# A fused transformer kernel: prologue written out, V's first half read later in its quarter, the attended rows' read signalled in halves

## The reference

```python
x = x + 0.5 * ffn(layernorm(x))
x = x + attn(layernorm(x))      # two K and V sets, 16 heads of 8 channels, state = product of K^T V, linear in the sequence
x = x + 0.5 * ffn(layernorm(x))

def ffn(x):                     # 16 heads of 64, 8 experts, the best 2 chosen per row and head
    q, k = x @ Wq[h], x @ Wk[h]
    w, sel = top_k(x @ Ws[h], 2);  mix = one_hot(sel) * sigmoid(w)
    v = sum_e mix[h, e] * (x @ Wv[e])
    attended = softmax(q * scale @ k.T) @ v
    mask = one_hot(top_k(x @ Wd[h], 2))
    return sum_h sum_e mask[h, e] * (attended[h] @ Wo[e].T)
```

## Time and profile before

| | |
|---|---|
| median of 3 runs | 2392.2 us (2389.46 to 2398.71) |
| the profiled execution | 2388.17 us, span 2386.4 us |
| TensorE, matmuls | 2293.9 us busy (96%), 49920 |
| TensorE, weight loads | 2148.7 us (90%) |
| VectorE | 2060.7 us (86%) |
| ScalarE | 1950.4 us (82%) |
| GpSimd | 1161.0 us (49%) |
| DMA, mean | 163 GB/s |
| granted TensorE clock | 0.998 |

### The profile page before, as it was taken

The page is one execution under the profiler, slowest core; times in us unless marked ns, Lnnn a source line. Parts: engine busy times, 40 slices in busy tenths (PEclk is TensorE's granted clock), DMA queues, the critical chain, the costliest instruction groups (busy, mean ns, idle before and its releaser), DMA issues.

```text
span 2386.4 us, 120494 instructions
## 1 busy us (share of the span) xinstructions
PE 2293.9 (96%) x49920; PEld 2148.7 (90%) x49920; DVE 2060.7 (86%) x3755; ACT 1950.4 (82%) x6053; POOL 1161.0 (49%) x1190
## 2 busy tenths in 40 slices
PE   3999999999999999999999999999999999999997
PEld 3899898999999999999999999999999999999897
DVE  5888888989889898888989888888888888898884
ACT  2888787888888888888888888888888888888885
POOL 3445555455455454454454454454454454554431
PEclk9999999999999999999999999999999999999999
DMA  4555555655555555556556556556556555556553
GB/s 122 160 171 154 147 161 149 171 164 169 163 164 170 167 168 168 161 164 174 162 166 173 162 164 178 163 164 173 166 165 175 162 168 165 169 163 172 161 166 103
DMA packets 660701, 388.23 MB, mean 163 GB/s; under 512 B 232512, under 2 KB 585664, under 8 KB 660160
## 3 DMA queue, kind: packets, MB, share of 16 engines
q1 hardware_dynamic: 659728, 379.67, 55.0%
q10 hardware_dynamic: 432, 0.85, 0.1%
HBM read 191.64 MB, written 188.74 MB: 159 GB/s over the span
## 4 chain that ended last, share of the span: by engine, by line
PE 86%; ACT 6%; issue 4%; DVE 2%; POOL 1%; DMA 0%; SPq 0%; ACTq 0%; DVEq 0%; POOLq 0%
PE psT L477 19%; PE psS L432 15%; PE psT L494 8%; PE psT L496 6%; PE psT L495 6%; PE psS L524 6%; PE psT L524 6%; PE psT L445 6%; PE psT L489 5%; PE psT L459 5%; ACT PB L812 5%; ACT PJ L853 1%; DVE NMAX L693 1%; PE psT L603 1%; PE psT L530 1%
## 5 line engine op out<-in xcount | busy, mean ns | idle before, releaser
L812 ACT ACTIVATE PB<-psS,NMAX 128x256 f32<-128x256 f32 x2048 | 943.5, 488 | 101.4 <-DVE NMAX L693 101.4
L477 PE MATMUL psT<-V,PT 128*64 128x64 f32 x16384 | 544.3, 224 | 22.9 <-issue 22.2
L477 PEld LDWEIGHTS psT<-V,PT 128*64 128x64 f32 x16384 | 505.3, 138 | 51.7 <-issue 26.5
L812 ACT ACTIVATION_READ_ACCUMULATOR PB<-psS,NMAX 128x1 f32 x2048 | 452.8, 221 | 0.0
L761 DVE TENSOR_TENSOR QK<-psT,QK 128x512 fp32r<-128x512 f32 x512 | 349.0, 688 | 119.0 <-ACT QK L820 112.4
L432 PE MATMUL psS<-QK 64*128 64x256 f32 x6144 | 442.8, 288 | 3.1 <-DVE PT L765 2.6
L820 ACT ACTIVATE QK<-psT 128x512 fp32r<-128x512 f32 x512 | 307.3, 602 | 164.8 <-PE psT L496 141.0
L432 PEld LDWEIGHTS psS<-QK 64*128 64x128 f32 x6144 | 393.5, 187 | 8.3 <-issue 4.7
L693 DVE TENSOR_REDUCE NMAX<-psS 128x2 f32<-128x512 f32 x512 | 329.6, 685 | 51.5 <-PE psS L432 48.1
L927 POOL TENSOR_TENSOR BT<-MT,diagv 128x1024 f32<-128x1024 f32 x128 | 304.5, 2379 | 110.4 <-DMA MT<-MIXd 106.3
L933 POOL TENSOR_TENSOR MB<-MASKT,diago 128x1024 f32<-128x1024 f32 x128 | 250.2, 1956 | 144.3 <-DVE GM L770 116.4
(11 more groups left out here) (121 smaller groups left out, 4777.9 us busy)
## 6 DMA issues: line engine op xcount, KB each, us to landing
Vd<-VM SPq DMA_DIRECT2D x512, 128.0 KB, 2.3
V<-Vd SPq DMA_DIRECT2D x512, 128.0 KB, 3.1
AOd<-AO SPq DMA_DIRECT2D x256, 256.0 KB, 2.7
AR<-AOd SPq DMA_DIRECT2D x256, 256.0 KB, 4.1
PJd<-PJ SPq DMA_DIRECT2D x64, 512.0 KB, 2.8
PR<-PJd SPq DMA_DIRECT2D x256, 128.0 KB, 2.5
MIXd<-MIX SPq DMA_DIRECT2D x64, 128.0 KB, 2.3
MT<-MIXd SPq DMA_DIRECT2D x64, 128.0 KB, 3.3
```

The costliest lines, as they stand in the source:

```text
L477: last = eng.matmul(M[64 * u:64 * u + 64, (t * NT + it) * DH:(t * NT + it + 1) * DH], PT[:, t, jt, cols], V[:, pm % 2, 4 * r + t, jt, :], ...
L812: eng.activation(PB[:, ab, j, it, :], psS[:, ab, j, it, :], ACT.Exp, bias=NMAX[:, ab, j, it:it + 1], accum_out=SUM[:, p % 2, it, 4 * r + t ...
```

## The change

Three things. First, the loops start at quarter 0, and each engine has the prologue written out in an order of its own (`AHEAD` gives the banks; 16 items, as before). Each constant has its own semaphore, the first inputs and weights are read ahead of the others, the work of sequences 0 to 2 is interleaved with the rounding of weights, and the first projections stand ahead of the first values. In GpSimd's prologue the mask's step comes after the mix. Second, in the fourth quarter SyncE's queue stores V's second half first, then waits for the product that TensorE computes in this quarter, reads V's first half, stores AO and then reads PR. Third, `s_ar` becomes two semaphores, one for each half of AR's four reads, and each half of `expand` waits for its own. New functions (`gates`, `choose`, `choose_second`, `store_mix` and others) hold the code that stood in the loops.

```diff
-        QUARTERS = range(-12, total + 6)
+        QUARTERS = range(total + 6)
...
+        AHEAD = [("xturn", 0), ("gates", 0), ("expert", 0, 0), ("expert", 0, 1), ("xturn", 1), ("gates", 1), ("qk", 0), ("qk", 1), ("xturn", 2),
+                 ("values", 0, 0, 0), ("values", 0, 0, 1), ("expert", 1, 0), ("values", 0, 1, 0), ("values", 0, 1, 1), ("expert", 1, 1), ("gates", 2)]
+        place = {item: k for k, item in enumerate(AHEAD)}
...
-            eng.dma_start(raw_g, WgT).then_inc(s_const, 16)
-            eng.dma_start(raw_q, WqT).then_inc(s_const, 16)
-            for dst, src in ((diagv, diagv_d), (diago, diago_d), (ramp, ramp_d), (headmask, heads_d), (awq, aWq), (awkv, aWkv), (awo, aWo)):
+            eng.dma_start(raw_g, WgT).then_inc(s_gload, 16)
+            eng.dma_start(ramp[:], ramp_d).then_inc(s_gload, 16)
+            eng.dma_start(X[:, 1].rearrange("p n c -> p (n c)"), x_rows(x, 1)).then_inc(s_x[1], 16)
+            eng.dma_start(raw_q, WqT).then_inc(s_qload, 16)
+            eng.dma_start(X[:, 2].rearrange("p n c -> p (n c)"), x_rows(x, 2)).then_inc(s_x[2], 16)
+            for dst, src in ((diagv, diagv_d), (diago, diago_d), (headmask, heads_d), (awq, aWq), (awkv, aWkv), (awo, aWo)):
                 eng.dma_start(dst[:], src).then_inc(s_late, 16)
...
+            eng.dma_start(X[:, 3].rearrange("p n c -> p (n c)"), x_rows(x, 3)).then_inc(s_x[3], 16)
...
+            store_experts(0)
+            load_experts(0)
+            store_mix(0, 3)
+            load_mix(0)
+            store_values(0, 0)
+            store_values(0, 1)
+            load_values(0, 0)
+            load_values(0, 1)
+            store_experts(1)
+            load_experts(1)
+            store_mix(1, SHARES + 3)
+
             for n in QUARTERS:
                 p, r = divmod(n, 4)
-                if r == 0 and runs(p):
+                if r == 0 and runs(p) and p >= 1:
...
-                    q = p + 2
-                    wait_freed(eng, "expert", q, 0)
-                    wait_freed(eng, "expert", q, 1)
-                    if q >= 2:
-                        eng.wait_ge(s_pr, 16 * PARTS * (q - 1))
-                    eng.dma_start(PJd[q % 2].rearrange("(p x) -> p x", p=P),
-                                  PJ[:, :, :, :].rearrange("p e n d -> p (e n d)")).then_inc(s_pjw, 16)
+                    store_experts(p + 2)
                 if r == 2 and runs(p + 1):
                     store_values(p + 1, 0)
                 if r == 3 and runs(p + 1):
+                    store_values(p + 1, 1)
+                    wait_full(eng, "product", n - 1)
                     load_values(p + 1, 0)
-                if r == 3 and runs(p + 2):
-                    q = p + 2
-                    eng.wait_ge(s_pjw, 16 * (q + 1))
-                    for a in range(2):
-                        wait_full(eng, "values", q - 1, 1, a)
-                    stored = PJd[q % 2].rearrange("(g r x) -> r g x", r=P, x=NT * DH)
-                    for i in range(PARTS):
-                        own = slice(8 // PARTS * i, 8 // PARTS * (i + 1))
-                        eng.dma_start(PR[:, own, :], stored[:, own, :]).then_inc(s_pr, 16)
-                if r == 3 and runs(p + 1):
-                    store_values(p + 1, 1)
                 if works(n - 1):
                     m = n - 1
                     wait_freed(eng, "product", m)
                     if m >= 8:
-                        eng.wait_ge(s_ar, 16 * PARTS * (m // 4 - 1))
+                        for b in range(2):
+                            eng.wait_ge(s_ar[b], 8 * PARTS * (m // 4 - 1))
                     eng.dma_start(AOd[m // 4 % 2].rearrange("(p r x) -> p r x", p=P, r=4)[:, m % 4, :], AO[:, m % 2, :]).then_inc(s_aow[m % 2], 16)
+                if r == 3 and runs(p + 2):
+                    load_experts(p + 2)
                 if r == 0 and runs(p - 1):
                     q = p - 1
                     eng.wait_ge(s_maskw, 16 * (q + 1))
...
-                        eng.dma_start(AR[:, own, :], stored[:, own, :]).then_inc(s_ar, 16)
+                        eng.dma_start(AR[:, own, :], stored[:, own, :]).then_inc(s_ar[2 * i // PARTS], 16)
                 if r == 3 and runs(p + 2):
-                    q = p + 2
-                    eng.wait_ge(s_share, SHARES * (q + 1))
-                    if q >= 2:
-                        eng.wait_ge(s_mt, 16 * (q - 1))
-                    eng.dma_start(MIXd[q % 2].rearrange("(p x) -> p x", p=P),
-                                  MIX[:, :, :, :].rearrange("p e n h -> p (e n h)")).then_inc(s_mixw, 16)
+                    store_mix(p + 2, SHARES * (p + 3))
...
-                if b == 0:
-                    eng.wait_ge(s_ar, 16 * PARTS * (q + 1))
+                eng.wait_ge(s_ar[b], 8 * PARTS * (q + 1))
                 eng.wait_ge(s_mb[b], q + 1)
...
+                if q < 2:
+                    eng.wait_ge(s_split, 2)
+                    wait_freed(eng, "xturn", q)
...
+            turn_x(0)
+            gates(0)
+            expert(0, 0)
+            expert(0, 1)
+            turn_x(1)
+            gates(1)
+            project(0)
+            project(1)
+            turn_x(2)
+            values(0, 0)
+            expert(1, 0)
+            values(0, 1)
+            expert(1, 1)
+            gates(2)
             for n in QUARTERS:
...
+            wait_x(eng, 0)
+            statistics(s_stat, 0, 0, x_of(0))
+            eng.wait_ge(s_gload, 32)
+            eng.tensor_copy(rampb[:, :], ramp[:, :]).then_inc(s_resid)
+            remainder(1, raw_g, wg)
+            remainder(2, raw_v, wv)
+            wait_x(eng, 1)
+            eng.wait_ge(s_xn, 2)
+            statistics(s_stat, 4, 0, x_of(1))
+            remaining_x(0)
+            remainder(3, raw_q, wq)
+            copy_gates(0)
+            eng.wait_ge(s_resid, 1)
+            choose(0)
+            choose_second(0)
+            remaining_x(1)
+            wait_x(eng, 2)
+            eng.wait_ge(s_xn, 4)
+            statistics(s_stat, 8, 0, x_of(2))
+            remainder(4, raw_k, wk)
+            copy_gates(1)
+            choose(1)
+            remaining_qk(0)
+            remaining_qk(1)
+            remaining_x(2)
+            choose_second(1)
+            eng.wait_ge(s_ident, 16)
+            eng.wait_ge(s_late, 16 * 14)
             eng.tensor_tensor(awq[:, :], awq[:, :], ident[:, :], ALU.add).then_inc(s_resid)
             for i in range(4):
                 eng.tensor_tensor(awkv[:, i * C:(i + 1) * C], awkv[:, i * C:(i + 1) * C], ident[:, :], ALU.add).then_inc(s_resid)
-            eng.tensor_copy(rampb[:, :], ramp[:, :]).then_inc(s_resid)
             eng.tensor_scalar(headmask[:, :], headmask[:, :], SSCALE, None, ALU.mult).then_inc(s_resid)
+            copy_gates(2)
...
+            round_weights(s_gload, 32, raw_g, wg)
+            round_weights(s_vload, 16, raw_v, wv)
+            round_x(0)
+            round_weights(s_qload, 16, raw_q, wq)
+            copy_expert(0, 0)
+            copy_expert(0, 1)
+            round_x(1)
+            round_weights(s_kload, 16, raw_k, wk)
+            sigmoid(0)
+            rounded(-1, 0)
+            rounded(-1, 1)
+            round_x(2)
+            sigmoid(1)
+            copy_values(0, 0)
+            copy_expert(1, 0)
+            copy_values(0, 1)
+            copy_expert(1, 1)
             for n in QUARTERS:
                 p, r = divmod(n, 4)
                 if r == 3 and runs(p + 2):
...
+            normalise_x(0)
+            normalise_x(1)
+            first_shares(0)
+            normalise_x(2)
+            eng.wait_ge(s_late, 16 * 14)
+            spread_mix(0, 0)
+            spread_mix(0, 1)
+            first_shares(1)
```

More of the change, by code:

```diff
@@ L216, in macaron_kernel @@
                 place[item] = len(place)
-        s_const = semaphore("s_const")
+        s_ident = semaphore("s_ident")
+        s_gload = semaphore("s_gload")
+        s_vload = semaphore("s_vload")
+        s_qload = semaphore("s_qload")
+        s_kload = semaphore("s_kload")
         s_late = semaphore("s_late")
@@ L227, in macaron_kernel @@
         s_vw = [semaphore(f"s_vw{i}") for i in range(2)]
+        s_ar = [semaphore(f"s_ar{i}") for i in range(2)]
         s_aow = [semaphore(f"s_aow{i}") for i in range(2)]
@@ L335, in load_values, with store_experts, load_experts @@
                     eng.dma_start(loaded[:, own], stored[:, own]).then_inc(s_value[q % 2], 16)
+            def store_experts(q):
+                wait_freed(eng, "expert", q, 0)
+                wait_freed(eng, "expert", q, 1)
+                if q >= 2:
+                    eng.wait_ge(s_pr, 16 * PARTS * (q - 1))
+                eng.dma_start(PJd[q % 2].rearrange("(p x) -> p x", p=P),
+                              PJ[:, :, :, :].rearrange("p e n d -> p (e n d)")).then_inc(s_pjw, 16)
+            def load_experts(q):
+                eng.wait_ge(s_pjw, 16 * (q + 1))
+                for a in range(2):
+                    wait_full(eng, "values", q - 1, 1, a)
```

(54 more changed lines are left out.)

91 lines of the change are left out of this document (49 added, 42 removed).

## The result

| | before | after |
|---|---|---|
| median (4 runs each, one chip) | 2394.65 us | 2475.43 us (2471.84 to 2490.85) |
| ratio | 1 | 1.0356, 95% interval 1.0317 to 1.0394 |
| profiled span | 2386.4 us | 2473.7 us |
| first score product | 53.71 | 40.15 |
| from there to pass 10 | 373.66 | 386.13 |

The account below looks back on a forecast made before the run. TensorE was taken as the bound, its matmuls covering 2293.9 of 2386.4 us. Prologue -18.4, queue -17.3 and end -1.8 summed to -37.5 us, giving 2355 us against the median 2392.2; range 2343 to 2375.

Parts of the forecast that it names:

- first scores: Prologue: the first score product starts at 36.1 us instead of 53.71, -17.6 us.
- the rest up to pass 10: Prologue past the first score product: -2.6 us for the first product's wait for V, +1.8 for a new wait.
- fourth quarters: Loop: stops in fourth quarters go, 17.1 us from the 13 quarters and 3.7 from four others.
- new traffic, third quarters: Loop: moved reads and AR's tail run over other packet borders, towards the third quarter's short blocks; +3.5 us.
- end, split semaphore: End: the first expand half runs while AR's second half lands, -1.8 us (0 to -1.9).
- late packets: Loop: TensorE's stops without a semaphore are instruction packets that queued behind data, chiefly the read of V's first half.
- while that holds: Loop: later V, AR, MT and masks cost 0 while their delays stay hidden behind TensorE's 35.5 us a pass.
- E's place: Second quarter of each pass: TensorE waits for V's late second half in 62 passes; slower, 2413 us, chance 0.05.
- Rival D: Loop: AR's tail and PJ's store meet short blocks, each fourth pass pays 1 us at two borders; 2381 us, chance 0.07.
- The new wait of 1.8 us: Prologue: the third quarter's values product waits for the second sequence's spreading, after a late MIX store; 1.8 us (0 to 4).
- The 1.6 us to spare for V: Prologue: V's second half lands at 43.9 us, the first product wants it at 45.5.
- rival B: Fourth-quarter queue edit gives nothing, as the packet is late for another reason or at another border; 2372 us, chance 0.22.

Follow-up runs that it names:

- the first of the two kernels: Kernel after with the old fourth-quarter list, and in SyncE's prologue store_experts(1) moved ahead of both reads of V; 2379.48 us, ratio 0.9931.
- Short spreadings: Kernel after, but from pass 4 on GpSimd's spreadings into BT and MB write a quarter of their elements (work left out); 2450.84 us, ratio 1.024.
- both causes away: Kernel after, but from pass 4 on a quarter of AR's rows read and a quarter of BT's and MB's elements spread (work left out); 2379.77 us, ratio 0.9948.

## Why the prediction was wrong

| term | forecast | measured |
|---|---|---|
| first scores | -17.6 | -13.6 |
| the rest up to pass 10 | -0.8 | +12.5 |
| fourth quarters | -20.8 | -13.4 |
| new traffic, third quarters | +3.5 | +87.7 |
| GpSimd late, second quarters | 0 | +14.6 |
| end, split semaphore | -1.8 | -0.5 |

- **The cause was read rightly.** The stops are late packets; V's first half brings the fourth quarter's; reading it later takes 13 of 21 us away. The 8 us that stay lie at the same border, the quarter's 261st to 263rd instruction (before, the 265th to 267th).
- **The step that failed is the price of the late list.** The slip itself was worked out nearly: V's second half 3.3 us later (measured 3.9), MT and AR 2 to 3 (4.3 and 3.8). Its cost was put at 0 "while that holds" and at 3.5 us for new traffic; it measured 87.7 us in third quarters and 14.6 in second ones. It was right that TensorE did not wait for V's second half or for AR in the loop, so E's place is innocent. Wrong was to look only at who waits for the data, and not at what its bytes run into: in the third quarter scores, values, product and expand pass so quickly that the 256 instructions ahead of a border there take as little as 3.3 to 3.8 us, against 5.7 on a pass's mean.
- **Rival D was one of the two mechanisms**, with 0.07 and 30 us; GpSimd's is not in it. Its size was off twice: three borders of four passes are hit, not two, with stops of 2.0, 1.4 and 1.5 us on the mean, up to 3.9; and a stop can cost more than its length (below). The longest such stop in the loop of before was 1.7 us (the 2.6 of the earlier trace rows is the first product's wait of the earlier trace rows); that alone should have put D's price above 1 us a border.
- **GpSimd was not weighed.** MT had "1 to 3" us of slack and slipped by 4.3, and the masks came late too: GpSimd waited 77.5 us for MASKT ahead of MB's spreading, before 27.1. That spreading then fell onto VectorE's choice: in after it overlaps EQ 37 of 64 times, which then takes 1.80 us on the mean, without a spreading beside it 0.69; in before it never does. Waits of GpSimd were counted, what it does to VectorE was not.
- **Prologue.** The first scores came 4 us late. F and GM took 4.2 us more than undisturbed, by the same collision; VectorE's chain was costed at its length alone. With QK's remainders ahead of them the scores began at 37.88, 2.3 us earlier than in after and 1.1 earlier than in the first of the two kernels; the rest of the 4 us is not shown to be the collision's. The new wait of 1.8 us was not the one that came: PJ's store behind V's reads cost 5 us, since the forecast looked for who waits for the *second* MIX and not for who needs PJ free. The 1.6 us to spare for V seem to hold in after by luck: V was there at 50.4 and not at 43.9, but TensorE came later still. Without PJ's stop the first product waited 1.04 us. Of the 12.5 us up to pass 10 about 6 are the late list's too: with the old order the stretch took 380.07 us.
- **Split semaphore.** -1.8 assumed that the first expand half runs while the second half lands. It does, but the stretch behind pass 60 was only 0.5 us shorter in after and 0.8 longer in the kernel with this edit alone; the forecast left out that the second half is waited for too, 0.82 us, and what the clock does behind such stops.
- The Trainium skill, "Runtime: NRT & Kernel Launch", section "Instruction fetch mechanics", which spoke against the change (rival B), is not borne out: crossing a block is "mostly hidden" there, and here it stopped TensorE for 18 us of the loop of before and 61 of after.

## What to carry over

A long instruction stream shares the DMA engines with the data, so a transfer's place matters even if nobody waits for it: before moving one, look where its bytes will run and how many microseconds a packet's instructions last there. In one in-order queue, an issue put ahead of another brings its wait along; everything behind slips by it. Of two causes that overlap, take both away before pricing either: 25 and 34 us alone were 96 together.

## What the runs showed of the hardware

- **Some long stops of TensorE are followed by its lower clock.** Short spreadings, pass 48, behind a stop of 2.7 us that began at 1868.7 (from:to, length, PE, PEld, DVE, ACT, POOL, granted clock, DMA share, GB/s):

```profile
1870.00:1872.00 2.00, 0.60 (x12) 0.60 (x14) 0.24 (x1) 1.38 (x7) 1.80 (x3) 0.84 0.78 233
1872.00:1874.00 2.00, 2.00 (x42) 2.00 (x42) 0.38 (x1) 0.00 (x0) 0.00 (x0) 0.50 0.32 91
1874.00:1876.00 2.00, 2.00 (x58) 1.93 (x54) 1.00 (x2) 0.00 (x0) 0.00 (x0) 0.81 0.35 131
```

  The granted clock falls to 0.50 (1.2 of 2.4 GHz) about when TensorE is back at work, and 42 matmuls pass in 2 us. In the loop of after this followed six of the ten longest stops (those ten took 2.2 to 3.9 us each). Over that loop the same matmuls were busy 1836.4 instead of 1816.1 us. Of these 20 us, 10.8 lie in the six third quarters with the lower clock; the rest lies at 1.00, as it does where a quarter of AR is read (1831.2 us busy, no stretch at the lower clock in the loop). With both causes away it was 1813.6. So the clock has some 11 of the loop's 89 us.
- **VectorE with two SBUF inputs is held up beside GpSimd's spreading**: F 0.69 to 2.88 us, EQ 760 to 1335 ns on the mean. With an input in PSUM it does not (QK 1.28 us for two, with the spreading beside it and without). The Trainium skill, "SBUF — State Buffer", section "Who interferes with whom", says that a VectorE instruction with two SBUF inputs contends with a GpSimd instruction that reads SBUF, and one with at most one SBUF input does not; the trace agrees.
- **Packets go on waiting behind data**: with V's read in their way, or AR's, TensorE broke off inside a run of matmuls for 0.2 to 3.9 us, at the same place of the program every fourth pass. The Trainium skill, "Runtime: NRT & Kernel Launch", section "Instruction fetch mechanics", calls the crossing mostly hidden; here the product alone stopped for 12 to 60 us of a kernel's loop, and the measurement decides.
- Open: what delays the packet in those of the 13 fourth quarters (8 or 9 of them) that still stop when V's read is late or small; what makes the matmuls busy 9 to 15 us longer at full clock where GpSimd runs late; and why the third quarter of pass 1 of four never stops at a packet's border.
